# Decoder block on one core: negated row maxima reach the transposed queries by SyncE transfers, and the parts of the self-attention pass run in another order

## The reference, cut to what matters

```python
x = x + _L1_attn_ref(_layernorm(x), w_qkv, w_proj, q_gamma, q_beta, k_gamma, k_beta)
# inside: 16 heads of width 16
q, k, v = split(x @ w_qkv)
q, k = layernorm(q) * q_gamma + q_beta, layernorm(k) * k_gamma + k_beta    # per head
att  = softmax(q @ k.T / 4)                                                 # per head, 256 x 256
out  = (att @ v) @ w_proj
```

## Time and profile before

| what | value |
|---|---|
| median of three runs | 2810.4 us |
| profiled execution | 2814.0 us, of which the span is 2812.2 us |
| PE busy over the span | 2412.6 us, 86% |
| DVE busy over the span | 1972.8 us, 70% |
| ACT busy over the span | 1556.4 us, 55% |
| POOL busy over the span | 1322.5 us, 47% |
| mean granted TensorE clock | 0.931 |
| attention pass, 984 to 1908 us: PE busy | 827.1 us of 924 us, granted clock 0.92 |
| attention pass: DVE, ACT, POOL busy | 718.5, 643.4, 393.0 us |

### The profile page before, as it was taken

One profiled execution on the slowest core, in us unless ns is written; L12 is line 12 of the kernel. 1 busy time (PEld: TensorE's weight loads), 2 busy tenths in 40 slices (PEclk: granted clock), 3 DMA queues, 4 the chain that ended last, 5 costly groups with the idle time before them and its releaser, 6 DMA issues. The chain is left out here.

```text
span 2812.2 us, 50061 instructions
## 1 busy us (share of the span) xinstructions
PE 2412.6 (86%) x16388; PEld 1898.8 (68%) x16388; DVE 1972.8 (70%) x4681; ACT 1556.4 (55%) x3048; POOL 1322.5 (47%) x1313
## 2 busy tenths in 40 slices
PE   5999999489999679999999999987998987799991
PEld 3666666379999545666666666655887776699991
DVE  4888888356565348888888888854777775577773
ACT  3777777345555237777777777663433432223443
POOL 5777777444443254444444444402565555002556
PEclk9999999689999879999999999888999998799996
DMA  2122222242221001010010101004332433446885
GB/s 70 61 76 72 64 76 59 59 138 96 64 85 40 25 19 31 28 31 27 31 35 27 31 27 31 24 20 137 100 121 98 154 111 107 151 139 183 254 251 179
DMA packets 215965, 234.34 MB, mean 83 GB/s; under 512 B 32623, under 2 KB 201841, under 8 KB 215457
## 3 DMA queue, kind: packets, MB, share of 16 engines
q1 hardware_dynamic: 194144, 184.75, 20.9%
q0 software_dynamic: 20480, 46.39, 5.5%
q10 hardware_dynamic: 1088, 0.00, 0.0%
HBM read 133.82 MB, written 101.25 MB: 84 GB/s over the span
## 5 line engine op out<-in xcount | busy, mean ns | idle before, releaser
L1348 POOL TENSOR_TENSOR f_hm<-f_hm,f_mhalf 128x64 f32<-128x64 f32 x32 | 347.2, 10851 | 2.7
L1528 DVE TENSOR_REDUCE f_nm<-f_raw 128x4 f32<-128x1024 f32 x256 | 311.1, 1215 | 32.4 <-PE f_raw L1649 32.3
L1421 ACT ACTIVATE f_PT<-f_sco 128x1024 f32<-128x1024 f32 x256 | 262.8, 1027 | 84.6 <-PE f_sco L1667 84.4
L2377 POOL DMA_INDIRECT d_pick<-expert_out,e_out_slots x128 | 139.2, 1088 | 259.2 <-DMA expert_out<-d_eo 156.3
L910 ACT ACTIVATE b_hT<-b_H,b_b1r 128x512 f32<-128x512 f32 x128 | 88.3, 689 | 163.3 <-PE b_H L1039 148.0
L2396 ACT ACTIVATE d_hh<-d_H 128x512 fp32r<-128x512 f32 x85 | 50.8, 598 | 211.4 <-PE d_H L2482 211.4
L1649 PE MATMUL f_raw<-f_k4T,f_q4T 64*128 64x256 f32 x1024 | 133.0, 340 | 33.4 <-DVE f_nm L1528 30.5
L1904 POOL DMA_INDIRECT expert_in<-g_xm,e_slots x128 | 131.1, 1024 | 40.2 <-issue 37.0
L1054 PE MATMUL b_O<-b_w2l,b_hTh 128*128 128x256 f32 x512 | 145.8, 285 | 0.0
L677 PE MATMUL a_bank<-a_w,a_xnT 128*128 128x512 f32 x256 | 126.5, 618 | 21.9 <-ACT a_xnT L394 21.9
L1054 PE MATMUL b_O<-b_w2h,b_hTh 128*128 128x256 f32 x512 | 144.8, 283 | 0.0
(11 more groups left out here) (370 smaller groups left out, 7838.8 us busy)
## 6 DMA issues: line engine op xcount, KB each, us to landing
d_xs<-expert_in SPq DMA_DIRECT2D x85, 256.0 KB
expert_out<-d_eo SPq DMA_DIRECT2D x85, 256.0 KB
x_scratch<-a_x SPq DMA_DIRECT2D x64, 256.0 KB, 2.2
b_w<-in_L_ffn_W_dram SPq DMA_DIRECT2D x16, 1024.0 KB
a_x<-in_x_dram SPq DMA_DIRECT2D x32, 256.0 KB
a_cx<-in_ctx_dram SPq DMA_DIRECT2D x32, 256.0 KB, 3.1
f_x<-x_scratch SPq DMA_DIRECT2D x32, 256.0 KB
f_xr<-x_scratch SPq DMA_DIRECT2D x32, 256.0 KB, 2.6
```

Source lines behind the costliest of these rows:

```text
L1348: g.tensor_tensor(hm[b % 2][:, :], hm[b % 2][:, :], mhalf[:, :], ALU.pow).then_inc(hroot, 1)
L1421: s.activation(PT[n % 3][:, t, :, :], heads(SCO), ACT.Exp, scale=float(DH) ** -0.5).then_inc(probs_ready, 1)
L1528: v.tensor_reduce(nm[:, t, g * HG:(g + 1) * HG], heads(RAW), AX.X, ALU.max, negate=True)\
L2377: g.indirect_dma_start(pick[b % GR][:, t, c, :], None, ex.eo_d[k], bass.IndirectOffsetOnAxis(ap=ex.out_slots[:, b, t, c:c + 1], axis=0), b ...
```

## The change

- The two `shift` copies into `q4T` (DVE L1542 and ACT L1412) go. SP issues two transfers for each row tile, four for each sequence, from `nmT` partitions 0 to 15 to partitions 0 to 15 and 64 to 79 of `q4T`; each moves 16 partitions x 8 blocks x 128 floats, 64 KB in runs of 512 bytes. `att 0` waits for all four by a DMA semaphore.
- `copy_max` goes, since only 16 transposed rows are needed; DVE's copy from PSUM to `nmT` shrinks to 16 partitions.
- `qk split5` is taken by ACT instead of DVE.
- `head_gamma` and `low` on DVE do both row tiles in one instruction: four instructions become two in each.
- SP follows ORDER: `load_x` stands at `in norm`, `load_xr` at `att 0`, the store at `out proj`, the new transfers at `raw shift0` and `raw shift1`.
- ORDER changes. At the end of a slot the sequence is now `raw 7, qk split7, att 7, qk split6, raw shift1, qk split3, att end`; at its start it is `qk scale, in stats, raw 0, att 0, raw 1, out o0, att 1, in norm, out o1, raw 2, att 2`. `in v` stands ahead of `raw 5`, and `qk high` comes after `out proj`.

```diff
         ORDER = (
-            "raw 0", "in stats", "att 0", "raw 1", "att 1", "out o0", "in norm", "out o1", "raw 2", "att 2",
-            "qk scale", "head var", "in normT", "qk gamma", "out oT", "att 3", "raw 3", "in qk0", "qk high",
-            "in qk1", "out proj", "raw max0", "raw 4", "qk low", "att 4", "raw shift0", "raw 5", "in v", "qk split0",
-            "att 5", "qk split1", "qk split2", "raw 6", "qk split3", "att 6", "qk split4", "qk split5", "att 7",
-            "raw 7", "raw max1", "qk split7", "qk split6", "raw shift1", "att end")
+            "qk scale", "in stats", "raw 0", "att 0", "raw 1", "out o0", "att 1", "in norm", "out o1", "raw 2",
+            "att 2", "head var", "in normT", "qk gamma", "out oT", "att 3", "raw 3", "in qk0", "in qk1", "out proj",
+            "qk high", "raw 4", "qk low", "att 4", "raw shift0", "in v", "raw 5", "qk split0", "att 5", "qk split1",
+            "qk split2", "raw 6", "att 6", "qk split5", "qk split4", "raw 7", "qk split7", "att 7", "qk split6",
+            "raw shift1", "qk split3", "att end")
-        on_dve = lambda r: r in (1, 5)
+        on_dve = lambda r: r in (1,)
# SP
+            def shift(t, b):
+                cols = slice(t * P, (t + 1) * P)
+                wait_taken(sync, f"raw shift{t}", b)
+                for at in (0, SL):
+                    sync.dma_start(q4T[b % 3][at:at + H, :, cols].bitcast(F32),
+                                   nmT[0:H, cols].bitcast(F32).unsqueeze(1).broadcast_to([H, NB, P]))\
+                        .then_inc(shift_in[b % 2], 16)
+            slots({"in norm": load_next, "att 0": load_xr, "out proj": store, **numbered("raw shift", shift, T)})
# ACT
-            def shift(t, b):
-                at, cols = slice(SL, SL + H), slice(t * P, (t + 1) * P)
-                wait_taken(act, f"raw shift{t}", b)
-                s.activation(q4T[b % 3][at, :, cols], nmT[at, cols].unsqueeze(1).broadcast_to([H, NB, P]), ACT.Copy)\
-                    .then_inc(shift_act, 1)
# DVE
-            def copy_max(t, b):
-                dve.wait_ge(raw_taken, b * FR + (t + 1) * NG)
-                v.tensor_copy(nm[:, t, SL:SL + H], nm[:, t, 0:H]).then_inc(nm_ready, 1)
             def shift(t, b):
-                v.tensor_copy(nmT[:, cols], bank[:, 0:P]).then_inc(taken(f"raw shift{t}"), 1)
-                wait_taken(dve, f"raw shift{t}", b)
-                v.tensor_copy(q4T[b % 3][0:H, :, cols], nmT[0:H, cols].unsqueeze(1).broadcast_to([H, NB, P]))\
-                    .then_inc(shift_dve, 1)
+                v.tensor_copy(nmT[0:H, cols], (A, Z)[t][0:H, 0:P]).then_inc(taken(f"raw shift{t}"), 1)
# PE
             def attend(k, b):
-                    pe.wait_ge(shift_dve, T * (b + 1))
-                    pe.wait_ge(shift_act, T * (b + 1))
+                    pe.wait_ge(shift_in[b % 2], 64 * (b // 2 + 1))
```

More of the change, by code:

```diff
@@ L1211, in attention_pass @@
         q4T, k4T = sbn("q4T", 3, [P, NB, S], F32R), sbn("k4T", 3, [P, NB, S], F32R)
-        nm, nmT = sb("nm", [P, T, P]), sb("nmT", [P, S])
+        nm, nmT = sb("nm", [P, T, P]), sb("nmT", [P, S], F32R)
         PT = sbn("PT", 3, [P, T, HG, S])
@@ L1226, in attention_pass @@
         raw_psum, raw_taken = sem("raw_psum"), sem("raw_taken")
-        nm_ready = sem("nm_ready")
-        shift_dve, shift_act = sem("shift_dve"), sem("shift_act")
+        shift_in = semn("shift_in", 2)
         scores_psum, probs_ready, probs_used = sem("scores_psum"), sem("probs_ready"), sem("probs_used")
@@ L1305, in _, with load_next @@
             load_x(1)
[L1306 to L1312, removed]
+            def load_next(b):
+                if b + 2 < B:
+                    load_x(b + 2)
+            def shift(t, b):
[6 more added lines that the diff above has]
+            slots({"in norm": load_next, "att 0": load_xr, "out proj": store, **numbered("raw shift", shift, T)})
             for u in range(2):
@@ L1391, in high @@
                 if b:
-                    wait_full(act, "qk split6", b - 1)
-                    wait_full(act, "qk split7", b - 1)
+                    for u in range(2):
+                        act.wait_ge(bank_full[u], 1 + max(use[f"qk split{r}", b - 1] for r in range(u, SRND, 2)))
                 for t in range(T):
@@ L1439, in _ @@
                 "in normT": take_xnT, **numbered("in qk", take_qk, T), "in v": take_v, "qk high": high,
-                **numbered("qk split", take_split, SRND), **numbered("raw shift", shift, T),
+                **numbered("qk split", take_split, SRND),
                 **numbered("att ", exps, FR), "att end": take_oT, "out oT": take_onT,
@@ L1504, in head_gamma @@
                     dve.wait_ge(scaled, 2 * b + 1 + k)
-                    for t in range(T):
-                        last = v.tensor_tensor(qk[b % 3][:, t, :, :], qk[b % 3][:, t, :, :], tile[:, :, :], op)
+                    both = qk[b % 3][:, :, :, :].rearrange("p t h d -> p t (h d)")
+                    last = v.tensor_tensor(both, both, tile[:, :, :].rearrange("p h d -> p (h d)").unsqueeze(1)
+                                           .broadcast_to([P, T, 2 * H * DH]), op)
                     last.then_inc(qk_ready if k else scaled, 1)
@@ L1510, in low @@
                 dve.wait_ge(high_ready, b + 1)
[L1511 to L1514, removed]
+                for n, (dst, at) in enumerate(((q4, 3 * DH), (k4, 2 * DH))):
+                    last = v.tensor_tensor(dst[:, :, :, at:at + DH], qk[b % 3][:, :, n * H:(n + 1) * H, :],
+                                           dst[:, :, :, DH:2 * DH].bitcast(F32), ALU.subtract)
                 last.then_inc(low_ready, 1)
@@ L1529, in raw_max @@
                     .then_inc(raw_taken, 1)
-            def copy_max(t, b):
-                dve.wait_ge(raw_taken, b * FR + (t + 1) * NG)
-                v.tensor_copy(nm[:, t, SL:SL + H], nm[:, t, 0:H]).then_inc(nm_ready, 1)
             def shift(t, b):
                 cols = slice(t * P, (t + 1) * P)
-                bank = (A, Z)[t]
                 wait_full(dve, f"raw shift{t}", b)
-                dve.wait_ge(shift_act, T * b)
-                v.tensor_copy(nmT[:, cols], bank[:, 0:P]).then_inc(taken(f"raw shift{t}"), 1)
-                wait_taken(dve, f"raw shift{t}", b)
-                v.tensor_copy(q4T[b % 3][0:H, :, cols], nmT[0:H, cols].unsqueeze(1).broadcast_to([H, NB, P]))\
-                    .then_inc(shift_dve, 1)
+                if b:
+                    dve.wait_ge(shift_in[(b - 1) % 2], 64 * ((b - 1) // 2 + 1))
+                v.tensor_copy(nmT[0:H, cols], (A, Z)[t][0:H, 0:P]).then_inc(taken(f"raw shift{t}"), 1)
             def take_o(t, b):
@@ L1563, in _ @@
                 "qk gamma": head_gamma, "qk low": low, **numbered("qk split", take_split, SRND),
-                **numbered("raw ", raw_max, FR), **numbered("raw max", copy_max, T), **numbered("raw shift", shift, T),
+                **numbered("raw ", raw_max, FR), **numbered("raw shift", shift, T),
                 **numbered("out o", take_o, T), "out proj": add_proj,
@@ L1641, in raw @@
                 if f == 0:
-                    wait_taken(pe, "qk split6", b)
-                    wait_taken(pe, "qk split7", b)
+                    for u in range(2):
+                        pe.wait_ge(bank_taken[u], 1 + max(use[f"qk split{r}", b] for r in range(u, SRND, 2)))
                 if b or f:
@@ L1654, in shiftT @@
                 wait_free(pe, f"raw shift{t}", b)
-                pe.wait_ge(nm_ready, T * b + t + 1)
+                pe.wait_ge(raw_taken, b * FR + (t + 1) * NG)
                 t_.transpose((A, Z)[t][:, 0:P], nm[:, t, :], ident[:, :]).then_inc(full(f"raw shift{t}"), 1)
```

## The result

The changed kernel takes 2796.8 us in the median of eight runs against 2812.7 us for the kernel before in eight runs on the same chips: ratio 0.9944, 95% interval 0.9933 to 0.9955, or 16 us less. Its profiled execution has a span of 2794.4 us against 2812.2 us.

What follows compares the result with a forecast made beforehand. PE was taken to bound the kernel, through its waits and low clock at the slot's start. Waits summed to −0.05 us a period, the clock to 23 us: 2814.0 − 23 − 32 x 0.05 = 2789.4, median forecast 2788, range 2768 to 2826.

Steps and rivals of the forecast that it cites:

- (e): Transfers of shift1 ahead of att 0: second landed 2.5 us after DVE's copy, inside the slack to 2.95, cost nothing.
- R3: Rival, more gained: DVE's freed 3 us bring reductions earlier, 25.1 us a period, no long ones; 2757, half 2770; chance 0.15.
- (a): PE's 0.62 us wait ahead of shift1 goes, covered by split7, att 7 and split6: gain 0.6 us a period, bounds 0.4 to 0.62.
- (b): New PE wait at split3, until DVE has copied shift1 out of bank Z: loss 0.45 us a period, bounds 0.3 to 0.7.
- (c): raw 1 still waits for DVE's reduction of raw 0, 0.95 us against 0.74: loss 0.2 a period, bounds 0 to 0.4.
- (d): out o0 covers att 1's 0.24 us wait, att 2 comes closer to its exponential: gain 0.1 a period, bounds 0 to 0.24.
- R2: Rival, slower: shift1's second transfer lands late, att 0 holds PE 0.45 us a period, more low clock; 2833 us; chance 0.24.
- (f): Mid-slot reordering of in v, qk high and split5, where PE is never idle: cost 0.
- (g): Low clock after the slot's start: 6 instead of 17 of 23 periods long, 17 us plus 6 us gained; bounds 0 to 35.
- R1: Rival, clock unchanged: waits exchanged, PE's dent as deep, as many low stretches; 2809 us, between 2804 and 2814; chance 0.19.

Runs made afterwards that it cites:

- the kernel without transfers: Changed kernel without the shift transfers and the waits for them, maxima not subtracted, everything else done: 2761.0 us, ratio 0.9825.
- the third transfer: Changed kernel with one more narrow transfer of the same size, issued by SP ahead of shift1's two and waited for with them: 2836.1 us, ratio 1.0094.
- the runs with filling matmuls: Useless matmuls: eight ahead of att 0 in changed kernel, 2780.7 us; six ahead of raw 1 in kernel before, 2776.4; those six plus raw 7 moved, split5 on ACT, 2788.5.
- each half alone: Changed kernel with new order but maxima copied by DVE and ACT: 2821.3 us; with transfers but the old order, four gamma and low instructions: 2883.5 us.
- the wide one: Changed kernel plus a 64 KB transfer over 128 partitions into a spare tile, issued by ACT beside SP's first of shift1: 2812.4 us in one execution.

## Why the prediction was right, and where it was not

The median of 2796.8 lies in the range and on the forecast side, 9 us above the 2788 forecast. The sum itself gives less than the forecast: 2789.4 less the 3.6 us between profile and median is 2785.8. And its upper bound of 26.5 us a period holds nothing for (e), whose 0.45 us would make it 26.9. In R3, half of the gain of 54 us would give 2783, not 2770. By its steps:

(a) The wait ahead of shift1 goes: right; the row of shift1 has no idle.

(b) The new wait of split3 for bank Z: right in place, 0.37 us against 0.45.

(c) raw 0 to raw 1: walked as 1.85 us from start to start; it is 1.84, and 1.83 without the transfers, where raw 1 is released by DVE's reduction. The chain copy, scaling, statistics, reduction is as long as walked. In the changed kernel itself PE's wait stands at att 0, and raw 1 has none.

(d) att 1 and att 2: wrong. A gain of 0.1 was taken; att 1 waits 0.27 us, because att 0 is late, and att 2 another 0.16, together 0.43 against 0.24 before. The kernel without transfers has 1.02 us from raw 1 to att 1 and no wait in between.

(e) The transfers: a mis-sized term. I had an issue of 0.36 us and 2.1 us to land, 2.5 us after DVE's copy for the second; it was 0.60 to 0.64 and 2.3, so 3.02 us, at the edge of the slack of 2.95. And the slack was counted for raw 1 alone: att 0's exponential, on which att 1 hangs, had none. Its price is 0.34 us a period where I had nothing. By the sign that I had set down for R2 (att 0 is PE's longest wait, raw 1 has none) R2 came true, and yet the kernel isn't slower. Without the transfers the kernel takes 36 us less, so R2's price of 23 us was too small rather than too large; the new order gives back more than that. That the landing decides from there on, the third transfer shows.

The Trainium skill, "DMA: Bandwidth & Descriptors", section Anatomy of one DMA, gave an estimate of 2.15 us to land for a transfer issued from GpSimd; SP's transfers here landed after 2.3. The Trainium skill, "SBUF — State Buffer", section Door 1: The DMA port swizzle, gave an estimate of 0.6 us of moving for each and a landing at 3.1 to 3.3 us: the two needed 1.4 us of packets, 0.7 each, and 3.0 us, so its number was the nearer one. That its mechanism is the cause is not shown.

(f) The middle of the slot: right, the waits of PE between 1150 and 1750 us name only split3, att 0 and the exponential at att 1 and att 2.

At full clock the waits come to 1.80 us (0.37, 1.00, 0.27, 0.16) against 1.60, and the period to 25.9 us against 25.73, where the sum had 25.7. Off DVE's busy time came 2.5 us a sequence, not 3.0, and off ACT's 1.3, not 1.5; nothing hung on that.

(g) The clock: right in sign, two thirds of its size. 13 of 26 intervals are long, against 21 before; I had a quarter. In the 26 intervals the clock gave back 14 us and the longer full-clock period took 4 of them. The reason that I gave falls: the dent is not milder, PE is busy for 2.1 instead of 2.34 of 3.40 us. That long intervals are fewer was measured; why, given a deeper dent, is open. Since the forecast gain hung almost wholly on this step, that it came out on the right side is luck as far as my argument goes. That PE's idle time at the slot's start is a necessary part of the fall, the runs with filling matmuls show; that it is not enough, the kernel without transfers.

In the last five intervals I had 6 us for the clock, and they took 6.9 us less. The work taken off DVE and ACT is not needed to explain it: the kernel before with nothing but the filling matmuls needs 107.3 us there, and the new order with the copies kept needs 105.9, as the changed kernel does; the clock is at its lower level for 17 and 13 us of them, against 34 before and 20 after. The 4.5 us more up to the first store had no term, and their cause is open.

Of the rivals, R1 is out (the interval excludes no change) and R3 is out (the period is not 25.1 us).

## What to carry to other kernels

Before valuing relief of an engine, ask who ends last at each wait; here 2.5 us a period off DVE became DVE's idle time. Two transfers in place of a copy needed 3.0 us from the producer to the consumer here, and were to be had cheaply only with other work in between: change the order with them, or leave them, for each half alone was a loss. And where PE waits for 0.7 to 1 us in a regular place and rows show the clock at 1.2 GHz behind it, try a few idle matmuls into a bank that is overwritten anyway: inside the wait they left the full-clock period as it was, and brought 16, 35 and 9 us here.

## What the runs showed that I had not expected

- The issue of a transfer over 16 partitions x 8 repeats holds SP for 0.60 us, against 0.36 for a load of 256 KB, and the load of xr issued right behind takes 0.59 in place of 0.36; the wide one takes ACT 0.49:

```profile
1240.79 0.59 SPq L1297 DMA_DIRECT2D f_xr<-x_scratch  x1
```

- Two such transfers issued from two engines at the same moment are served largely one after the other (packets from 1.25 to 2.12 and from 1.81 to 2.63 us), no sooner than two issued by SP in a row.
- PE time that computes nothing can be worth more than PE time saved: some 0.65 us of filling matmuls took a period of 27.27 us to 25.73.
- The long interval comes after a dent in some slots and not in others with the same rows.
